# Layer 1 of a block's own edges as two half-height matmuls in two PSUM banks

## What is computed

```python
h = jnp.maximum(_layernorm(x, axis=-1), 0.0)
row, col = (edge_idx[0], edge_idx[1])          # row = src, col = dst
h = jnp.concatenate([h[row], h[col]], axis=-1) # one row of 128 features per edge
h = jax.nn.softplus(h @ W0 + b0)               # 128 -> 128
h = jax.nn.softplus(h @ W1 + b1)               # 128 -> 128
h = h @ W2 + b2                                # 128 -> 64
x = x + jax.ops.segment_sum(h, row, num_segments=x.shape[0])
```

## Time and profile before

| | us |
|---|---|
| median of 3 runs (2077.76 to 2082.0) | 2078.18 |
| the profiled execution | 2061.28 |
| its span in the trace | 2059.1 |
| of this: up to 313 (survey, `prepare`) | 313 |
| 313 to about 1280: `edges0` | about 965 |
| then `edges1` and `finish` | about 780 |

### The profile page before, as it was taken

One profiled execution on the slowest core, in us unless ns is written; L12 is line 12 of the kernel. 1 busy time (PEld: TensorE's weight loads), 2 busy tenths in 40 slices (PEclk: granted clock), 3 DMA queues, 4 the chain that ended last, 5 costly groups with the idle time before them and its releaser, 6 DMA issues. The chain is left out here.

```text
span 2059.1 us, 37167 instructions
## 1 busy us (share of the span) xinstructions
PE 1484.0 (72%) x10067; PEld 1099.1 (53%) x10067; DVE 1071.9 (52%) x3261; ACT 975.9 (47%) x2261; POOL 1098.6 (53%) x1151
## 2 busy tenths in 40 slices
PE   0033337999999999999999999346555556555656
PEld 0022225777777777777777777224333334433434
DVE  4899992555455555555555555236334433444344
ACT  0277884666666766666666666012111111111144
POOL 0499974444444444544444442676666666666600
PEclk9999999999999999999999999667777777777765
DMA  1355543443434434434434433322222222222159
GB/s 31 76 116 122 127 99 80 104 108 88 115 97 98 116 92 102 116 82 113 109 87 115 106 89 82 69 47 65 53 48 51 53 53 52 47 53 52 35 165 335
DMA packets 428697, 187.85 MB, mean 91 GB/s; under 512 B 381769, under 2 KB 407766, under 8 KB 428650
## 3 DMA queue, kind: packets, MB, share of 16 engines
q1 hardware_dynamic: 336168, 129.09, 24.4%
q0 software_dynamic: 28224, 32.57, 8.2%
q10 hardware_dynamic: 64258, 25.65, 4.3%
HBM read 131.42 MB, written 55.79 MB: 91 GB/s over the span
## 5 line engine op out<-in xcount | busy, mean ns | idle before, releaser
L805 POOL DMA_INDIRECT fast_gathered<-h_table,fast_gather_i x441 | 437.3, 992 | 524.3 <-PE bank L941 367.4
L1141 POOL DMA_INDIRECT fast_gathered<-h_neighbours_table,fast_index_i x441 | 423.9, 961 | 198.4 <-issue 178.3
L1041 ACT ACTIVATE fast_h<-bank,b_s 128x384 f32<-128x384 f32 (+1 forms) x490 | 302.0, 623 | 244.1 <-PE bank L953 169.3
L1202 PE MATMUL node_sums<-twice,fast_self_rows 128*64 128x128 f32 x784 | 135.9, 414 | 265.1 <-DMA fast_gathered<-h_neighbours_table,fast_index_i 261.5
L1202 PEld LDWEIGHTS node_sums<-twice,fast_self_rows 128*64 128x64 f32 x784 | 117.0, 216 | 305.0 <-issue 305.0
L1233 ACT ACTIVATE fast_z_in<-node_sums 128x512 f32<-128x512 f32 x49 | 29.3, 597 | 525.2 <-PE node_sums L1208 287.5
L1048 ACT ACTIVATE fast_h<-fast_h 128x384 f32<-128x384 f32 (+1 forms) x490 | 263.0, 557 | 0.0
L837 DVE TENSOR_TENSOR fast_message<-bank,b_s 128x192 f32<-128x192 f32 x147 | 52.5, 357 | 354.7 <-PE bank L988 296.8
L1187 DVE BATCH_NORM_STATS2 z_stats<-z_t (+1 forms) x48 | 33.3, 694 | 370.9 <-ACT z_t L1244 302.6
L967 PE MATMUL bank<-fast_h,w_s 128*128 128x384 f32 (+1 forms) x490 | 221.8, 534 | 0.5 <-ACT fast_h L1048 0.5
L1208 PE MATMUL node_sums<-fast_hot,fast_gathered 128*64 128x256 f32 (+1 forms) x980 | 207.8, 418 | 19.2 <-issue 19.2
(11 more groups left out here) (232 smaller groups left out, 2671.6 us busy)
## 6 DMA issues: line engine op xcount, KB each, us to landing
fast_local<-local_rows SPq DMA_DIRECT2D x49, 576.0 KB
h_neighbours_table<-fast_h_rows SPq DMA_DIRECT2D x49, 320.0 KB
fast_self_rows<-h_neighbours_table SPq DMA_DIRECT2D x49, 320.0 KB
h_table<-prep_normed ACTq DMA_DIRECT2D x49, 256.0 KB, 2.8
fast_own_rows<-h_table SPq DMA_DIRECT2D x49, 256.0 KB
x_plus_h<-fast_total SPq DMA_DIRECT2D x49, 256.0 KB
finish_resid<-x_plus_h SPq DMA_DIRECT2D x49, 256.0 KB
prep_xin<-in_x SPq DMA_DIRECT2D x48, 256.0 KB
```

The source lines that it names most:

```text
L805: pool.indirect_dma_start(gathered[slot][:, j * D:(j + 1) * D], None, h0_t, bass.IndirectOffsetOnAxis(ap=gather_i[q][:, n:n + 1], axis=0))\
L1041: A(to[at][:, 0:w], psum[:, 0:w], ACT.Exp, bias=b_s[:, :]).then_inc(done, 1)
L1141: pool.indirect_dma_start(gathered[q][:, c * MW:(c + 1) * MW], None, h1_t, bass.IndirectOffsetOnAxis(ap=index_i[q][:, c:c + 1], axis=0))\
L1202: nc.tensor.matmul(banks[6 + q % 2][h * D:(h + 1) * D, k * P:(k + 1) * P], self_rows[q][:, at:at + D], twice[:, :], start=(k == 0), stop=F ...
```

## The change

The own weight loses its zero half: `w0_own` is 128 x 128, with the summed weight in rows 0 to 63 and again in rows 64 to 127. Layer 1 of both own units is now done in step 0 by two matmuls of 64 rows and 512 columns: rows 0 to 63 (even sub-blocks, now own unit 0) into `ps_1`, rows 64 to 127 (odd sub-blocks, now own unit 1) into `ps_in`. They use half of the array's rows each (tile form 64 x 128). Their columns are copied first from `h0_cols` to the buffer `own_cols` by a DMA on SP's queue, one of 256 KB for each block. Since `ps_in` is now busy with own unit 1, `turn_rows` of far 0 waits for the exp of that unit, and stands at the end of step 1, behind merge of far 1'. In step 2 layer 1 of far 0 stands behind layer 2 of own 1. The last lines of the diff make exp of own 1 read `ps_in`, and `layer3` of an own unit write every second sub-block.

```diff
-        w0_own = sb("w0_own", [128, 2 * HID])
+        w0_own = sb("w0_own", [128, HID])
...
-                V.memset(w0_own[:, :], 0.0).then_inc(s_own, 1)
...
-                for h in range(2):
-                    half = slice(h * D, (h + 1) * D)
-                    V.tensor_tensor(w0_own[half, h * HID:(h + 1) * HID], w0_parts[0][half, :], w0_parts[1][half, :],
-                                    ALU.add)
+                V.tensor_tensor(w0_own[:, :], w0_parts[0][:, :], w0_parts[1][:, :], ALU.add)
...
+                own_cols = t("own_cols", [128, TW], 1)[0]
...
+                        def load_cols(b, q, turn):
+                            wait_from(sp, pre1_done, NU * (b - 1) + UNITS.index(("own", 1)) + 1, passed_sp)
+                            sp.dma_start(own_cols[:, :], h0_cols[:, bass.ds(b * TW, TW)]).then_inc(cols_loaded, 16)
...
-                        rounds(sp, [(0, load_rows), (0, load_local), (LAG + 2, store_h1), (LAG + 2, store_x1), (1, load_x)], BLOCKS, 2)
+                        rounds(sp, [(0, load_rows), (0, load_cols), (0, load_local), (LAG + 2, store_h1), (LAG + 2, store_x1), (1, load_x)], BLOCKS, 2)
...
                                 wait_from(pe, in_ready, GK * b + k)
+                                wait_from(pe, exp1_done, NU * b + UNITS.index(("own", 1)) + 1)
...
+                        def layer1_own(b, q, turn):
+                            wait_from(pe, exp1_done, NU * b)
+                            wait_from(pe, in_ready, GK * b)
+                            pe.wait_ge(cols_loaded, 16 * (b + 1))
+                            for k, to in enumerate((ps_1, ps_in)):
+                                half = slice(k * D, (k + 1) * D)
+                                M(to[:, 0:TW], w0_own[half, :], own_cols[half, :],
+                                  start=True, stop=True).then_inc(pre1_done, 1)
...
-                                else:
-                                    w = HALF // 2 * P
-                                    for h in range(2):
-                                        last = M(ps_1[:, h * w:(h + 1) * w], w0_own[:, h * HID:(h + 1) * HID],
-                                                 h0_cols[:, bass.ds(b * TW + k * w, w)], start=True, stop=True)
...
-                                        col = (j % 2 * (HALF // 2) + j // 2) * P
-                                        to = sub_at(k * HALF + j)
-                                        last = M(node_sums[q][:, to:to + D], h2[at][:, col:col + P], w2_s[:, :],
-                                                 start=(j == 0), stop=False, skip_group_check=True)
+                                        to = sub_at(2 * j + k)
+                                        last = M(node_sums[q][:, to:to + D], h2[at][:, j * P:(j + 1) * P], w2_s[:, :],
+                                                 start=(k == 0 and j % (HALF // 2) == 0), stop=False, skip_group_check=True)
...
-                            out = [(0, layer1(i)), (1, layer2(unit(1)))]
-                            if is_far(unit(-1)):
+                            out = [(1, layer2(unit(1)))]
+                            if i == 0:
+                                out.insert(0, (0, layer1_own))
+                            elif i == 2:
+                                out.append((0, layer1(i)))
+                            elif is_far(i):
+                                out.insert(0, (0, layer1(i)))
+                            if is_far(unit(-1)) and i != 1:
                                 out.append((-1, turn_rows(unit(-1))))
                             out.append((2, layer3(unit(2))))
                             if is_far(unit(3)):
                                 out.append((3, merge(UNITS[unit(3)][1])))
+                            if i == 1:
+                                out.append((-1, turn_rows(unit(-1))))
...
-                            out = [(0, exp(i, ps_1, b0_s, pre1_done, pre2_done, h1, exp1_done)),
+                            out = [(0, exp(i, ps_in if UNITS[i] == ("own", 1) else ps_1, b0_s, pre1_done, pre2_done, h1, exp1_done)),
```

More of the change, by code:

```diff
@@ L165, in gnn_program @@
         s_cz, s_ci, s_w, s_pm = sem("const_zeroed"), sem("const_made"), sem("weights_loaded"), sem("pair_mean_made")
-        s_gz, s_own = sem("diagonal_zeroed"), sem("own_weights_made")
+        s_gz = sem("diagonal_zeroed")
         s_wd = sem("diagonal_loaded")
@@ L218, in _ @@
                 dve.wait_ge(s_w, 16 * 18)
-                dve.wait_ge(s_own, 1)
-                for h in range(2):
-                    half = slice(h * D, (h + 1) * D)
-                    V.tensor_tensor(w0_own[half, h * HID:(h + 1) * HID], w0_parts[0][half, :], w0_parts[1][half, :],
-                                    ALU.add)
+                V.tensor_tensor(w0_own[:, :], w0_parts[0][:, :], w0_parts[1][:, :], ALU.add)
                 V.tensor_scalar(w0_up[:, :], w0_s[:, :], 0.0, None, ALU.max).then_inc(s_up, 1)
@@ L713, in edges0 @@
                                                                 "local_loaded"))
+                cols_loaded = s("cols_loaded")
                 dst_hot_ready, x_ready = s("dst_hot_ready"), s("x_ready")
@@ L948, in body @@
                                 kind, k = UNITS[i]
-                                if is_far(i):
-                                    pe.wait_ge(in_ready, GK * b + k + 1)
+                                pe.wait_ge(in_ready, GK * b + k + 1)
                                 wait_from(pe, exp1_done, NU * b + i)
-                                if is_far(i):
-                                    last = M(ps_1[:, 0:FW], w0_s[:, :], in_t[(GK * q + k) % 2][:, :], start=True, stop=True)
-                                else:
-                                    w = HALF // 2 * P
-                                    for h in range(2):
-                                        last = M(ps_1[:, h * w:(h + 1) * w], w0_own[:, h * HID:(h + 1) * HID],
-                                                 h0_cols[:, bass.ds(b * TW + k * w, w)], start=True, stop=True)
+                                last = M(ps_1[:, 0:FW], w0_s[:, :], in_t[(GK * q + k) % 2][:, :], start=True, stop=True)
                                 last.then_inc(pre1_done, 1)
```

## The result

| | us |
|---|---|
| kernel before, median in the comparison (2077.76 to 2084.19, 4 runs) | 2080.09 |
| changed kernel, median (2040.92 to 2045.06, 4 runs) | 2042.59 |
| ratio, 95% interval | 0.9824 (0.981 to 0.9838) |
| profiled execution, before and after | 2061.28, 2044.01 |
| span of its trace, before and after | 2059.1, 2042.4 |

The change makes the kernel faster. The median falls by 37 us, where the prediction had 9; the two profiled executions differ by 17 us. Why these two distances are not the same is a question of its own, taken up with the experiments.

The account below looks back on a forecast made before the run. PE was taken to set the pace, busy 777.0 of 779.8 us. Its own work -0.90 plus waits 0.39 and 0.32 gave -0.19 us per block, x 49 = -9 us: 2069 us, own range 2052 to 2076, 8 in 10 2040 to 2100.

Parts of the forecast that it names:

- wait A: PE at layer 2 of own 0 waits for ACT's ln of own 0: 0.39 us per block, bounds 0.20 and 0.82.
- wait B: PE at layer 1 of far 0 waits for ACT's take_in: 0.32 us per block, between 0.17 and 0.46.
- PE's own gain: PE's own work per block falls by 0.74 + 0.16 = 0.90 us of 19.4, if it waits for nothing.
- the step from the trace to the median: Runs' median lies 17 us over the profiled execution, the difference is the same: 2052 in the trace becomes 2069.
- The pair streams side by side: The two own matmuls on PE overlap fully, as in turn_rows: 0.86 us of streaming instead of 1.71.
- Changing the shape of the tiles: At the own pair on PE: 0.17 to fill and leave plus 0.05 to enter; pair costs 1.08, saves 0.74 us.
- The new order in PE's own work: Groups beside turn_rows change: layer 2 of own 0 saves 0.05, L988 of far 2' saves 0.11 us per block.
- late blocks: In 12 of 40 blocks ACT's exp of far 2' comes later, adding 0.3 x 0.62 us to PE's wait.
- Rival R4: ACT's exp of far 2' in step 0 late in every block: +0.38 us per block, +19 us, 2097; chance 0.14.
- Rival R1: PE's waits for ACT don't come, all 0.90 us per block is kept: -44 us, 2034; chance 0.12.
- Work with one answer: SP's later transfers (some 4 us), the own columns' copy, the pair's other waits and `setup` savings all cost or gain nothing.
- The sum: Per block -0.90 + 0.39 + 0.32 = -0.19 us, x 49 = -9 us.

Follow-up runs that it names:

- b_fourth: The kernel before, unchanged, run again on a third chip of the follow-up runs: 2061.66 us, ratio 1.0003, span 2061.6.
- b_again: The kernel before, unchanged, run again for a trace beside the changed kernel of 2018.82: 2039.07 us, ratio 0.9998.

## Why the prediction was right in direction and wrong in size

The forecast was faster, by 9 us; the median fell by 37.5, and by 21 to 23 in the four repetitions. The measured time of 2042.59 lies in the wide range (2040 to 2100) but below the forecast's own (2052 to 2076). The direction came out, and so did the overlap that makes it; the size did not. The step that failed first is that of the waits: the prediction took 0.39 + 0.32 = 0.71 us per block, and the runs show 0.225, all of it wait A; wait B isn't there. The second is PE's own gain, 0.90 in the prediction and 0.57 in the runs, which hid two thirds of that error. The third is the step from the trace to the median. By step:

**The pair streams side by side: right.** 0.86 was taken from turn_rows; the second tile on the same rows adds 0.852 (1.911 - 1.059), and on other rows none of it. That leaves 0.207 of the 1.059 for filling and leaving, against the 0.17 from turn_rows.

**Changing the shape of the tiles: too small.** The step "The pair costs 0.86 + 0.17 + 0.05 = 1.08" put the whole price inside the pair. The pair itself takes 1.059, but the group ahead pays 0.094 to enter (0.614 to 0.708) and the group behind 0.104 (0.645 to 0.749). The argument that matmuls of 64 columns have half of the entry paid already was wrong: they pay it in full. The prediction had the second number in its hands: it read that layer 3 behind turn_rows costs 0.72 and elsewhere 0.61, and used it as a gain of the new order, but not as a loss behind the pair. In all, 1.257 and not 1.08: +0.18. In the run with full rows both extra prices are gone. The Trainium skill ("TensorEngine Tiling (Array Packing)", Key Properties) says that changing the tiling mode drains the engine; the trace agrees, with 0.09 ahead and 0.10 behind.

**The new order in PE's own work: -0.16 predicted, 0.00 measured.** Layer 3 of far 2' does fall by 0.104, layer 2 of own 0 falls by 0.051 once its wait is out (0.952 to 0.901). What was left out is who stands at those places now: merge of far 1' ahead of turn_rows pays 0.094, layer 1 of far 0 ahead of the next turn_rows 0.050 more, and layer 2 of own 1, directly behind a turn_rows, 0.963. The places by the shape changes keep their price whoever stands there. The run with full rows confirms the sum.

**Wait A: 0.39 predicted, 0.225 measured.** Its short form was right in mechanism and place: layer 2 of own 0 starts at the end of ln of own 0 in all blocks but the first of 48, and no longer with the square moved. From layer 2 of far 2' to layer 2 of own 0 it takes 942.42 - 939.80 = 2.62 in the changed kernel at 2018.82, against the 2.60 worked out. The wait shows as 0.164 in merge's distance, against 0.20, and as 0.061 in layer 2's own, which the sum didn't have. The part that failed is the 0.3 x 0.62 for late blocks: the row "ACT fast_h L1041 <- PE bank L988" has a counterpart in b_fourth (6.5, 11, 0.6) and none in b_again, so it goes with the higher level and not with the kernel. In the changed kernel's first trace ACT's waits read:

```profile
ACT fast_h L1052 <- PE bank L962: 120.9, 122, 1.8
ACT fast_h L1052 <- PE bank L954: 12.7, 37, 0.3
ACT fast_h L1052 <- PE bank L971: 4.3, 5, 1.2
```

No line for L991 (layer 3) is among them, and merge of far 0' has a mean of 1.33 there against 1.29 on the regular chip: at this place the lateness costs 0.04 and not 0.19. Rival R4, which made it the rule, is out. As a whole the higher level does cost 0.26 us in a block (19.48 against 19.22), but the changed kernel pays the same (19.13 against 18.87), so nothing of it enters the difference.

**Wait B: 0.32 predicted, none measured.** The step "take_in of far 0 starts 934.44 - 932.50 = 1.94 after its turn_rows" read a delay as if it belonged to the transfer of the result. It belonged to ACT's queue: the exp and ln of own 1 stood ahead of it. In b_again take_in (L1033) follows the first half of ln with no idle time in brackets:

```profile
921.19 0.62 ACT L1048 ACTIVATE fast_h<-fast_h 128x512 f32<-128x512 f32 x1
921.74 0.49 ACT L1033 ACTIVATE fast_in_t<-bank 128x384 f32<-128x384 f32 x1
```

In the changed kernel ACT is idle for 1.9 us before it, and starts 946.80 - 945.45 = 1.35 after turn_rows began. PE and ACT in the changed kernel at 2018.82, in order of time:

```profile
945.45 0.32 PE L937 MATMUL bank<-ident,fast_gathered 128*64 128x128 f32 x1
...
946.80 0.49 ACT L1044 ACTIVATE fast_in_t<-bank 128x384 f32<-128x384 f32 x1 [1.91 <-PE bank L943]
...
947.65 0.81 PE L962 MATMUL bank<-fast_in_t,w_s 128*128 128x384 f32 x2
```

From the start of turn_rows to layer 1 of far 0 stand 2.20 us, and turn_rows (1.242) with layer 2 of own 1 (0.963) fill them: no wait is left. The lower bound, from the 1.65 of far 2, was too high as well. Here are turn_rows of far 2 and its take_in in b_again and then in b_fourth:

```profile
930.31 0.32 PE L935 MATMUL bank<-ident,fast_gathered 128*64 128x128 f32 x1
...
931.66 0.49 ACT L1033 ACTIVATE fast_in_t<-bank 128x384 f32<-128x384 f32 x1 [0.25 <-PE bank L941]
```

```profile
940.72 0.32 PE L935 MATMUL bank<-ident,fast_gathered 128*64 128x128 f32 x1
...
942.40 0.49 ACT L1033 ACTIVATE fast_in_t<-bank 128x384 f32<-128x384 f32 x1 [0.59 <-PE bank L941]
```

From start to start 1.35 on the one chip and 1.68 on the other, ACT idle and waiting for PE in both: these 0.3 us go with the level, and the trace of before is one of the second kind. Rival R1 was right for this wait and wrong for wait A; that 2042.59 lies not far from its 2034 is chance, since no trace shows the 0.90 that it keeps.

**Work with one answer: right.** SP's delay is there at the size foretold and costs nothing, as the run with the copy last shows.

**The sum.** Predicted -0.90 + 0.39 + 0.32 = -0.19. Measured -0.57 + 0.225 + 0 = -0.34, on the chips of 2039; in the first pair of traces -0.35. PE's own gain was put 0.33 too high, the waits 0.49 too high, and so two errors of opposite sign left a rest of half the true size. That the block foretold at 19.2 took 19.13 is luck to that extent. The sum had no term for the start of `edges0` either: the second block begins 3.7, 3.9 and 5.4 us earlier in the pairs of traces of the three sets that have both kernels, and 0.2 later in the first pair. The changed kernel's own traces differ there more (334.3 to 343.8 us), and no run isolates the cause.

**From the trace to the median.** "The median of the runs lies 17 us over that execution, the difference is the same" is a step of its own, and it failed. With the sum at its true size, -17, the trace's own time gives 2044, and the profiled execution of the changed kernel took 2044.01. The profiled execution of the kernel before isn't one of its timed runs, and their level of 2080 isn't the one that its trace shows; no run since has reached it. Of the 26 us by which the forecast missed, 8 are the sum's, the other 18 this step's. Why the kernel before stood 17 us over its trace and the changed kernel did not stays open. Where a profiled execution and the median lie 17 us apart, as here, that alone is a reason to keep both times, 2052 and 2069, as ends of the forecast's own range.

## What to carry to other kernels

Two matmuls of half the contraction height on different halves of the array streamed in the time of one here, but the change of tile shape has to be charged three times: inside the new group (0.2 us), to the group ahead (0.09) and to the one behind (0.10). In these traces that was the same for groups ahead of 64, 80 and 384 columns, and for groups behind of 64, 384 and 512. A gap between two instructions on another engine is a price only if that engine was idle in it; first look at what stood ahead in its queue, since the change may take just that away. Where a change makes the bounding engine arrive earlier, look in the waiting engine's list for work that nobody needs yet: to move one such instruction (the square) behind the needed one gave 9.6 and 11.2 us beside the change's own 22, and the kernel that has both is the one to keep.

## What the runs showed of the hardware

The unchanged kernel kept one level within each set of runs, with intervals of a tenth of a per cent, and another in other sets, each on a chip of its own: 2039, 2039, 2061 and 2062 us (and 2080 in the first comparison). None of these four sets shares its chip with another, so whether the level belongs to the chip or to the occasion isn't shown. Of the 25.9 us between b_again and b_fourth 12.1 show as blocks of 19.38 in place of 19.22 with two near 20 us every eleventh, the rest outside the blocks. The second of two 64-row matmuls of 512 columns in float32, on the other rows and into another bank, added no streaming (1.059 against 1.911 when both are on the same rows). Layer 2 of own 0 cost 0.06 us more from start to start when PE had waited for its operand than when it stood behind other work (0.962 against 0.901).
